# Attention block and 4-bit feed-forward block: turning the next rows off the tensor engine, and reordering what is summed when

## The reference

```
x = x + layernorm(attention(layernorm(x)))        16 heads of 128, causal softmax, W_Q W_K W_V W_O with biases
x = x + layernorm(ffn(layernorm(x)))              gate/up/down, hidden 2048, tanh GELU
weights of the ffn: 4-bit codes, two per integer, a table of 16 values, one scale per 32 values
attention: q, k, v = x W + b;  softmax(q k^T / sqrt(128)) v;  sum over heads of z W_O + b_O
```

## Time and profile before

| | |
|---|---|
| time, median of 3 runs | 1555.29 us (1555.06 to 1555.84) |
| the profiled execution's own time | 1557.55 us |
| its span, first to last instruction | 1555.8 us |
| mean granted TensorE clock | 0.999 |
| PE, DVE, ACT, POOL busy | 1539.1, 1080.1, 985.8, 714.2 us |
| transposes of the rows, `transpose_x` | 64, the first at 126.9 us, the last at 1009.3 us |
| DMA | 190.48 MB, mean 122 GB/s |

### The profile page before, as it was taken

One profiled execution on the slowest core, in us unless ns is written; L12 is line 12 of the kernel. 1 busy time (PEld: TensorE's weight loads), 2 busy tenths in 40 slices (PEclk: granted clock), 3 DMA queues, 4 the chain that ended last, 5 costly groups with the idle time before them and its releaser, 6 DMA issues.

```text
span 1555.8 us, 25706 instructions
## 1 busy us (share of the span) xinstructions
PE 1539.1 (99%) x8136; PEld 1326.5 (85%) x8136; DVE 1080.1 (69%) x3116; ACT 985.8 (63%) x2449; POOL 714.2 (46%) x1069
## 2 busy tenths in 40 slices
PE   8999999999999999999999999999999999999998
PEld 7888888888888888888888888888788888888887
DVE  5666777777777777677777777757667676675765
ACT  7887777767776777677777776654444444444443
POOL 6673455444455455445445445433333333333333
PEclk9999999999999999999999999999999999999999
DMA  5653444444444444444444444681211121112101
GB/s 161 185 163 101 141 153 136 137 152 146 146 150 139 143 145 154 140 138 147 144 141 142 146 142 148 213 309 63 94 51 60 54 68 39 57 55 68 54 28 41
DMA packets 173415, 190.48 MB, mean 122 GB/s; under 512 B 17888, under 2 KB 143840, under 8 KB 173280
## 3 DMA queue, kind: packets, MB, share of 16 engines
q1 hardware_dynamic: 173280, 188.84, 37.9%
HBM read 105.93 MB, written 82.84 MB: 121 GB/s over the span
## 4 chain that ended last, share of the span: by engine, by line
PE 87%; DMA 4%; ACT 3%; DVE 3%; SPq 2%; issue 1%; POOL 0%; DVEq 0%; ACTq 0%
PE fbank L790 15%; PE fbank L788 15%; PE fbank L789 15%; PE obank L788 7%; PE obank L790 7%; PE obank L789 7%; PE ubank L788 5%; PE ubank L790 5%; PE ubank L789 5%; PE ubank L813 3%; PE fbank L899 3%; DMA turned_scratch<-turned 2%; DMA back<-turned_scratch 1%; SPq L542 1%; ACT probs L674 1%
## 5 line engine op out<-in xcount | busy, mean ns | idle before, releaser
L1378 POOL TENSOR_TENSOR pT_lo<-back,pT_hi 128x512 fp32r<-128x512 f32 x128 | 165.9, 1296 | 284.0 <-ACT pT_hi L742 284.0
L788 PE MATMUL fbank<-xnT_hi,wqk_hi 128*128 128x512 f32 x640 | 249.8, 390 | 0.2 <-DVE xnT_lo L972 0.2
L790 PE MATMUL fbank<-xnT_hi,wqk_lo 128*128 128x512 f32 x640 | 249.4, 390 | 0.0
L789 PE MATMUL fbank<-xnT_lo,wqk_hi 128*128 128x512 f32 x640 | 249.4, 390 | 0.0
L1338 POOL TENSOR_SCALAR probs<-probs,rsum 128x128 f32<-128x128 f32 (+1 forms) x512 | 210.5, 430 | 11.4 <-DVE rsum L995 6.5
L685 ACT ACTIVATE w_raw<-fbank 128x512 f32<-128x512 f32 x128 | 76.6, 598 | 211.9 <-PE fbank L790 211.9
L987 DVE CUSTOM_DVE_ANT_0 probs<-ubank,mask 128x128 f32<-128x128 f32 (+1 forms) x512 | 156.3, 356 | 30.5 <-PE ubank L790 28.2
L1358 POOL TENSOR_TENSOR v_lo<-probs,v_hi 128x512 fp32r<-128x512 f32 x64 | 83.1, 1299 | 175.5 <-ACT v_hi L694 175.5
L655 ACT ACTIVATE zT_hi<-fbank,bias_v 128x512 fp32r<-128x512 f32 x128 | 87.6, 685 | 119.0 <-PE fbank L899 118.9
L1358 POOL TENSOR_TENSOR kT_lo<-probs,kT_hi 128x512 fp32r<-128x512 f32 x64 | 82.7, 1292 | 160.8 <-ACT kT_hi L694 160.8
L1110 DVE SCALAR_TENSOR_TENSOR probs<-w_raw,fbank 128x512 f32<-128x512 f32 x128 | 88.0, 688 | 97.9 <-ACT w_raw L689 94.8
(11 more groups left out here) (168 smaller groups left out, 4513.4 us busy)
## 6 DMA issues: line engine op xcount, KB each, us to landing
turned_scratch<-turned SPq DMA_DIRECT2D x128, 384.0 KB, 2.5
back<-turned_scratch SPq DMA_DIRECT2D x512, 96.0 KB, 2.2
w_raw<-in_w_pairs SPq DMA_DIRECT2D x28, 256.0 KB, 3.1
w_hi_scratch<-w_hi SPq DMA_DIRECT2D x48, 128.0 KB, 2.0
w_lo_scratch<-w SPq DMA_DIRECT2D x48, 128.0 KB, 2.0
x_res<-in_x SPq DMA_DIRECT2D x16, 256.0 KB, 3.0
wqk_hi<-w_hi_scratch SPq DMA_DIRECT2D x16, 256.0 KB, 5.8
wqk_lo<-w_lo_scratch SPq DMA_DIRECT2D x16, 256.0 KB, 5.9
```

Source lines behind the costliest of these rows:

```text
L788: nc.tensor.matmul(out, a[0], b[0], start=start, stop=False, skip_group_check=skip)
L789: nc.tensor.matmul(out, a[0], b[1], start=False, stop=False, skip_group_check=skip)
L790: return nc.tensor.matmul(out, a[1], b[0], start=False, stop=stop, skip_group_check=skip)
L1378: pool.tensor_tensor(lo[:].rearrange("p u b (a j) -> p (u b) a j", j=32), mem.back[m % 2][:, :, 0:2].rearrange("p a u b j -> p (u b) a j") ...
```

## The change

Five edits:

1. The entries `("xT", ...)` and `transpose_x` are gone. DVE turns the normalised next rows in blocks of 32 into `stream` (part 5 of `norm_next_x`, after head 8, in chunk 0 after head 10), SP stores them and fetches them back into `x_in` (`turn_next`, at j = 9, in chunk 0 at j = 11), and one entry `("next", c + 1)` in step j = 14, behind k, has ACT and DVE split them from there.
2. In the steps with j = 15 the entry `("out", n - 3)` comes first, ahead of q.
3. `load_res` moves from j = 9 to j = 1, beside `next_x`.
4. The statistics, normalisation and roots of the attention's outputs move: `X1_AT`, `X1_ROOTS` 10 to 11.
5. `spread` takes four operations in place of five; in the feed-forward's first chunk the last residual add (part 5 of `finish_y`) moves from m = 16 to m = 15.

```diff
@@ step_plan
     plan = [("q", n + 1), ("k", n + 1), ("T", n)]
     if n % HEADS == HEADS - 2:
-        plan += [("xT", 0)]
+        plan.insert(2, ("next", n // HEADS + 1))
     if n > 2:
         plan += [("out", n - 3)]
-    if n % HEADS == HEADS - 2:
-        plan += [("xT", 1)]
     if n > 1:
         plan += [("z", n - 2)]
     plan += [("pT", n - 1), ("scores", n + 1)]
+    if n % HEADS == HEADS - 1:
+        plan.insert(0, plan.pop(plan.index(("out", n - 3))))
@@ load_program
+    def turn_next(c):
+        sp.wait_ge(s.next_turned, 2 * c + 2)
+        if c:
+            sp.wait_ge(s.next_back, 64 * c)
+        sp.dma_start(rows_v..., mem.next_turned...).then_inc(s.next_sent, 16)
+        sp.wait_ge(s.next_sent, 16 * (c + 1))
+        for k in range(4):
+            sp.dma_start(mem.rows_back[32 * k:32 * k + 32]..., rows_v[:, :, k]...).then_inc(s.next_back, 16)
...
         fetch(n)
         if c and j == 5:
             turn_given(c - 1)
+        elif j == (9 if c else 11):
+            turn_next(c)
...
             if j == (1 if c else 5):
                 next_x(c, i)
-            elif c and j == 9:
-                load_res(c - 1, i)
+                if c:
+                    load_res(c - 1, i)
@@ scalar_program
+        elif kind == "next":
+            act.wait_ge(s.next_back, 64 * m)
+            act.wait_ge(s.full, nth(("k", n + 1)))
+            for kt in range(KT):
+                act.activation(mem.xnT[0][:, kt, :]..., mem.rows_back[:, :, :, kt, :]..., ACT.Copy).then_inc(s.next_hi, 1)
@@ tensor_program
-    def transpose_x(kt, bank):
-        for t in range(TT):
-            last = nc.tensor.transpose(bank[:, t * P:(t + 1) * P], mem.x_in[:, t, kt:D:KT], mem.ident[:])
...
             if kind == "q" and h == 0:
-                pe.wait_ge(s.lo, split(("xT", m // HEADS, KT - 1)))
+                pe.wait_ge(s.next_lo, KT * (m // HEADS))
@@ vector_program
+    def turn_next():
+        for t in range(TT):
+            last = dve.transpose(mem.next_turned[:, :, t]..., x_in[:, t, :]...)
+            if t % 2:
+                last.then_inc(s.next_turned, 1)
...
-        after(dve.tensor_scalar(mem.spread[:], mem.words[:], 0xF0, 12, ALU.bitwise_and, ALU.logical_shift_left))
-        after(dve.scalar_tensor_tensor(mem.spread[:], mem.words[:], 0xF, mem.spread[:], ALU.bitwise_and, ALU.bitwise_or))
+        after(dve.scalar_tensor_tensor(mem.spread[:], mem.words[:], 12, mem.words[:], ALU.logical_shift_left, ALU.bitwise_or))
...
-    X1_AT = {(3, "sum"): (-2, -1), (8, "sum"): (0,), (9, "mid"): (1, 2), (10, "sum"): (3,), (12, "sum"): (4,), (13, "mid"): (5, 6)}
-    NEXT_AT = {(2, "sum"): (0,), (4, "sum"): (1, 2), (5, "mid"): (3,), (6, "sum"): (4,)}
-    FIRST_NEXT_AT = {(6, "sum"): (0,), (8, "sum"): (1, 2), (9, "mid"): (3,), (10, "sum"): (4,)}
+    X1_AT = {(3, "sum"): (-2, -1), (9, "mid"): (0, 1), (10, "sum"): (2,), (12, "sum"): (3, 4), (13, "mid"): (5, 6)}
+    NEXT_AT = {(2, "sum"): (0,), (4, "sum"): (1, 2), (5, "mid"): (3,), (6, "sum"): (4,), (8, "sum"): (5,)}
+    FIRST_NEXT_AT = {(6, "sum"): (0,), (8, "sum"): (1, 2), (9, "mid"): (3, 4), (10, "sum"): (5,)}
...
+        elif kind == "next":
+            for kt in range(KT):
+                dve.wait_ge(s.next_hi, KT * (m - 1) + kt + 1)
+                dve.tensor_tensor(mem.xnT[1][:, kt, :]..., mem.rows_back[:, :, :, kt, :]..., mem.xnT[0][:, kt, :]..., ALU.subtract).then_inc(s.next_lo, 1)
...
-            finish_at = {10: (-1,), 13: (0, 1), 14: (2,), 15: (3, 4), 16: (5,)}
+            finish_at = {10: (-1,), 13: (0, 1), 14: (2,), 15: (3, 4, 5)}
```

More of the change, by code:

```diff
@@ L286, in blocks @@
             return view.rearrange("p (k t r i) -> p k t r i", t=TT, r=KT, i=BLK)
+        self.next_turned = blocks(self.stream[:].rearrange("p t d -> p (t d)"))
         self.rows_turned = blocks(backs[:].rearrange("p n a u b j -> p (n a u b j)")[:, 0:TT * D])
@@ L378, in __init__ @@
         self.pool = sem("pool_chain")
+        self.next_turned = sem("next_rows_turned")
+        self.next_sent = sem("turned_next_rows_stored")
+        self.next_back = sem("turned_next_rows_back")
+        self.next_hi = sem("next_rows_hi")
+        self.next_lo = sem("next_rows_lo")
         self.rows_turned = sem("rows_turned")
@@ L493, in next_x @@
         if c:
-            sp.wait_ge(s.full, nth(("xT", c, KT - 1)))
+            sp.wait_ge(s.next_lo, KT * c)
         else:
@@ L605, in turn_rows @@
             sp.wait_ge(s.rows_back, 64 * n)
+        else:
+            sp.wait_ge(s.next_back, 64 * NCH)
         sp.dma_start(rows_v.rearrange("a i k c -> (a i) k c"),
@@ L628, in load_program @@
             else:
-                sp.wait_ge(s.full, nth(("xT", NCH, KT - 1)))
+                sp.wait_ge(s.next_lo, KT * NCH)
             sp.dma_start(mem.x_in[:], chunk(x1_v, c + 1)).then_inc(s.x, 16)
@@ L737, in scalar_program @@
                 full(count, mem.zT[0][:], bank, mem.bias_v[:, h:h + 1]).then_inc(s.hi, 1)
-            else:
-                full(count, mem.xnT[0][:, m, :], bank).then_inc(s.hi, 1)
+        elif kind == "next":
+            act.wait_ge(s.next_back, 64 * m)
+            act.wait_ge(s.full, nth(("k", n + 1)))
+            for kt in range(KT):
+                act.activation(mem.xnT[0][:, kt, :].rearrange("p (t a i) -> p t a i", a=4, i=BLK),
+                               mem.rows_back[:, :, :, kt, :].rearrange("p a t i -> p t a i"),
+                               ACT.Copy).then_inc(s.next_hi, 1)
         elif kind == "pT":
@@ L803, in project @@
         last.then_inc(s.full, 1)
-    def transpose_x(kt, bank):
-        for t in range(TT):
-            last = nc.tensor.transpose(bank[:, t * P:(t + 1) * P], mem.x_in[:, t, kt:D:KT],
-                                       mem.ident[:])
-        return last
     def scores(u, i, b):
@@ L1063, in norm_next_x @@
             moments()
+        elif part == 5:
+            turn_next()
         else:
             dve.wait_ge(s.rstd, next_norm(c))
-            last = standardise(x_in, x_in, 2 * (part - 3))
-            if part == 4:
-                last.then_inc(s.xn, 1)
+            after(standardise(x_in, x_in, 2 * (part - 3)))
+    def turn_next():
+        for t in range(TT):
+            last = dve.transpose(mem.next_turned[:, :, t].rearrange("p k r i -> p r k i"),
+                                 x_in[:, t, :].rearrange("p (k j r) -> p r k j", r=KT, j=BLK))
+            if t % 2:
+                last.then_inc(s.next_turned, 1)
     def spread(n):
@@ L1075, in spread @@
             dve.wait_ge(s.w4, n)
[L1076 to L1079, removed]
+        after(dve.scalar_tensor_tensor(mem.spread[:], mem.words[:], 12, mem.words[:],
+                                       ALU.logical_shift_left, ALU.bitwise_or))
         dve.tensor_scalar(mem.words[:], mem.spread[:], 0x80008, 12, ALU.bitwise_and,
@@ L1164, in vector_program @@
                     extra(c, j, "sum")
-            else:
-                full(count, mem.xnT[1][:, m, :], mem.xnT[0][:, m, :], bank)
+        elif kind == "next":
+            for kt in range(KT):
+                dve.wait_ge(s.next_hi, KT * (m - 1) + kt + 1)
+                dve.tensor_tensor(mem.xnT[1][:, kt, :].rearrange("p (t a i) -> p t a i", a=4, i=BLK),
+                                  mem.rows_back[:, :, :, kt, :].rearrange("p a t i -> p t a i"),
+                                  mem.xnT[0][:, kt, :].bitcast(F32).rearrange(
+                                      "p (t a i) -> p t a i", a=4, i=BLK),
+                                  ALU.subtract).then_inc(s.next_lo, 1)
         elif kind == "T":
```

20 lines of the change are left out of this document (12 added, 8 removed).

## The result

The changed kernel takes 1592.37 us (median of 6 runs, 1589.88 to 1596.42); the kernel before took 1555.84 us beside it (6 runs, 1555.06 to 1557.55). The ratio is 1.0236, 95% interval 1.0223 to 1.0248: slower by 36.5 us, where 18.7 were forecast, and outside the range. TensorE's mean granted clock fell from 0.999 to 0.993; in the six timed executions it lay between 0.988 and 0.994, and the two slowest have the two lowest.

The account below looks back on a forecast made before the run. PE's own work, busy 1539.1 of 1555.8 us, was taken as the bound. Terms -7.9 + 17.5 + 6.4 + 1.5 + 2.6 - 1.4 = +18.7 us gave 1574.0 us, range 1562 to 1583 (own range 1568 to 1580).

Parts of the forecast that it names:

- the clock: PE's granted clock was expected to stay up behind the new waits, so it added nothing to the sum.
- SP's queue in chunk 0: turn_next at step 11 makes the send of step 12 some 3.3 us late, mostly hidden: +1.5 us, bounds 0 and 3.3.
- Transposes, -7.9: Removing the transposes from PE saves 0.99 us in each of 8 chunks, -7.9 us.
- The first wait: In j = 15 of chunks 0 to 6, out ahead of q waits 2.5 us for zT_lo: +17.5 us.
- The second wait: In j = 15 of chunks 0 to 6, scores wait 0.9 us for k's low part: +6.4 us.
- rival D: PE's granted clock falls after each new wait, 2 us lost behind each of seven: 1588 us, 3%.
- In chunk 7: turn_next at j = 9 delays six loads, and a send goes 1.7 us late: +2.6 us, bounds 1 and 6.
- DVE's new work at 0: Turns, moved statistics and roots, and spread's dropped operation lie beside PE's work: 0, bounds -1 and +3 us.
- Feed-forward, -1.4: The earlier residual add removes PE's 1.38 us wait for ACT in the feed-forward: -1.4 us, bounds -1.4 and 0.
- A: DVE gets through early, so out's wait for zT_lo is 1.5 us and not 2.5: +11.7, 1567 us, 12%.
- B: DVE finishes zT_lo 2.5 us sooner, so both waits shrink: -5.2, 1550 us with neither; 9%.
- C: Each turn_next of chunks 1 to 6 also makes the ring 2 us late: +12 more, 1586 us, 6%.

Follow-up runs that it names:

- experiment 2: The kernel before with only the second edit, out ahead of q in the steps with j = 15: 1575.78 us, ratio 1.0117.
- experiment 1: The kernel after without its second edit, out again behind q and k in the steps with j = 15: 1569.01 us, ratio 1.0072.
- experiment 8: As experiment 7, with POOL subtracting the second half of the rows' low part: 1559.56 us, ratio 1.0016.
- experiment 3: The kernel after, with ten 128x128 matmuls on PE ahead of out's wait in the steps with j = 15: 1585.83 us, ratio 1.0181.
- experiment 4: The kernel after, with DVE's zT_lo ahead of the masks in the steps with j = 14: 1581.11 us, ratio 1.0157.
- Experiment 5: As experiment 1, with turn_next at j = 12 in chunk 0 and, in chunk 7, six weight loads between its store and wait: 1563.82 us, ratio 1.0041.
- experiment 6: As experiment 5, with the rows' entry behind the turning of the probabilities: 1559.68 us, ratio 1.002.
- experiment 7: As experiment 6, with the normalisations and roots of the attention's outputs back at their old places: 1555.91 us, ratio 0.9993.
- experiment 10: The kernel before with the fifth edit alone (four operations in spread, last residual add one step sooner): 1555.81 us, ratio 0.9986.
- experiment 9: As experiment 7, with PE waiting for the rows' low part half by half in the first q: 1553.48 us, ratio 0.998.

## Why the prediction was wrong

**The direction and the mechanism of the two waits were right.** Moving out alone costs 18.3 us (experiment 2), and undoing it in the kernel after gives 23.4 back (experiment 1). I had put 23.9 on it. Two terms failed: the clock, put at nothing, and SP's queue in chunk 0, put too small.

**Transposes, -7.9: right** (-7.8). The 0.99 a chunk held (0.96 to 0.99 in all eight), and the records' 280 ns would have misled.

**The first wait, 2.5 each: right.** Idle are 2.43 us in six steps and 2.15 in chunk 0. The chain was as said: `kT_lo`, the rows, the turning, the masks, `zT_lo`. One term came out otherwise: the rows took 1.42 and not 1.29. With both operands now in SBUF, the first subtraction fell beside POOL's `w4_lo`, which ends at 261.78, and ended 0.55 behind it, at 262.33, the same distance as in experiment 8. In chunk 0, which unpacks no words, the pair takes 1.29, and it also starts 0.15 us sooner behind `kT_lo`, since ACT has no `w_hi` to write ahead of `xnT_hi`. POOL in the kernel after, DVE in its chunk 0:

```profile
261.04 0.74 POOL L1358 TENSOR_TENSOR w<-w,w_hi 128x256 f32<-128x256 f32 x1 [1.85 <-ACT w_hi L702]
```
```profile
133.14 1.29 DVE L1191 TENSOR_TENSOR xnT_lo<-x_in,xnT_hi 128x512 fp32r<-128x512 f32 x2
```

Experiment 8 shows that pairing in the open.

**The second wait, 0.9 each: right.** Idle are 0.77. From the start of z's last pair (272.33) to that of the scores (273.49) it is 1.16 where 0.22 is usual, so 0.94 by starts. The first wait is 2.60 by starts (262.97 to 265.69, where 0.12 is usual). Behind each wait the first matmul is another 0.1 slow (0.34 instead of 0.23 to the next start at 396.59). Together that is 3.76, forecast were 3.4. Seven of them are 26.0 against 23.9, 2.1 of the miss.

**The clock, put at 0: this is the step that failed first.** I had argued from the mean of 0.999 over waits of up to 1.6 us that a wait of 2.5 would leave the clock alone, and gave the fall 3%, as rival D. The rows of before held no idle stretch of that length in the middle of work, so they could not exclude it. It came in four of seven equal places, 1.5 us each, 6.0 in this execution. Experiment 3 takes it away: 6.5 us of the median. The other executions, at clocks down to 0.988, may have had more of it; the 4.0 us that the medians are further apart than the profiled executions fit that, but are not shown, since only one execution was profiled. Waits of 1.40 and 1.31 us in the same place did not bring it (experiments 2 and 4), but that is no safe length: in experiment 4 it fell behind 1.49 us in step 124, while 1.59 us in step 2 of the kernel before had left it alone. The Trainium skill, "TensorE: Matmul & The Clock Gate", Part 1, has the clock halved by idleness; the trace agrees, with 0.50 behind 2.43 us of it. Why only some of the equal waits brought it stays open. And the clock is not the whole miss: with these falls gone experiment 3 still takes 1585.83 us, above the range; most of what is left over the forecast there is chunk 0 and the price of the two waits.

**SP's queue in chunk 0, +1.5: too small, it was +4.7.** I had the `send` 3.3 us late (3.4 measured) and then hid half of it behind "two free banks". Nothing hid it: the banks moved the stall to v in step 14, where PE stood 2.80 us, and in this execution the clock fell there too. In experiment 1 PE waited as long (2.75 us) at the same place, the clock stayed at 1.00, and the step was 15.78 us against 16.55, still 3.9 over a step without transposes. The upper bound of 3.3, from the lateness of the `send` alone, was too low even so. Experiment 5 removes it. **In chunk 7**, +2.6 was forecast and 2.7 measured; in the same experiment 1.1 of it is left (7.75 and 7.33 us for steps 124 and 125).

**DVE's new work at 0: an answer that was right for the wrong reason.** All other steps together are 1.3 us longer, so 0 looks nearly right, by luck. Experiments 6 and 7 show that it was not hidden by spare time of DVE: the rows ahead of the turning cost 4.1 us, and the new places of the outputs' sums 3.8. In the kernel after a part of this lay under the new waits. The bounds of -1 to +3 for it held only as long as PE was late anyway.

**Feed-forward, -1.4: -0.7** in the profile of after, -1.1 in experiment 10. The wait fell to 0.25, not to zero.

Rivals A and B fell with the 2.43 us. C fell too: in the kernel after, the steps behind `turn_next` in chunks 1 to 6 are not 2 us longer. The forecast's own range ended at 1580, the recorded one at 1583, and what lies above it is mostly the clock and chunk 0.

What in the change is worth having: the transposes off PE (-7.8) and the fifth edit, if out stays where it was, the rows go behind the turning, the queue is kept clear, the sums go back to their places, and PE waits for the rows' low part by halves (experiment 9, -3.9 us). Of the -7.8 there, 2.0 us are lost again in the steps with j = 15 and 2.7 in steps 124 and 125. Of the 36.5 us lost, 23.4 came from the order of one entry.

## What to carry to other kernels

Price a wait on the bounding engine as idle time plus what its clock does afterwards, and ask whether the trace of before has any idle stretch as long as the new one; if it has none, it says nothing against a fall. A single stretch that left the clock alone says little too, since stretches of the same length at the same place did both here. An entry that looks like plain work may be the cover between a producer and two consumers: before moving it, list for each neighbour when its operand is ready. And take a big new wait out before calling the smaller edits free, since it hides them.

## What the runs showed of the hardware that was not expected

- The granted clock went to 0.50 for some 3 us behind an idle stretch of 2.43 us in four of six equal places of one execution and stayed at 1.00 in two. Behind one of 2.80 us it fell in the kernel after, and behind 2.75 us at the same place of experiment 1 it did not. Behind the first waits of 1.03, 1.31 and 1.40 us in experiments 2 and 4 it stayed in all fourteen places. Behind 1.49 or 1.50 us in step 124 it fell in one of four kernels (experiment 4) and stayed in three. In step 2, early in the attention, it fell behind 2.26 us (experiment 2) and 2.01 us (experiment 4) and stayed behind 2.04 us (the kernel after).
- A subtraction of 128x512 on DVE with both operands in SBUF took 1.60 us beside a subtraction of POOL, where two of them take 1.25 alone, and POOL's next one took 1.64 instead of 1.30 (experiment 8 against 7).
- In SP's queue the bounce through DRAM took 5.5 us in chunk 0, where 4.8 were forecast: from the store's issue to the first fetch it is 3.72 us (109.31 to 113.03), 1.02 of it the issue itself.
